# Decoder layer: VectorE turns the cross-attention keys in squares of 32, the scores contract over 32 partitions, and the attention loops are written out

## What is computed

```python
x = _layernorm(x + _L0_attn_ref(x, ...), axis=-1)      # a state-space mixer, 128 heads
x = _layernorm(x + _L0_xattn_ref(x, ctx_4096), axis=-1)
x = _layernorm(x + _L0_ffn_ref(x, ...), axis=-1)       # 512x512 base + top-2 of 8 low-rank experts
...
def _L0_xattn_ref(query, key):
    a = jnp.einsum('bqd,bkd->bqk', query, key)
    e = jax.nn.softmax(a, axis=-1)
    c = jnp.einsum('bqk,bkd->bqd', e, key)
    return c
```

## Time and profile before

| | us |
|---|---|
| median of 3 runs | 1640.62 (1637.20 to 1644.48) |
| the profiled execution | 1644.59 |
| its span, first to last instruction | 1642.8 |
| mean granted TensorE clock | 0.981 |

### The profile page before, as it was taken

How to read it: one execution, slowest core, us unless ns; L and a number is a source line. 1 busy time by engine, 2 the same in 40 slices (tenths; PEclk the granted TensorE clock), 3 DMA queues, 4 the chain that set the end, 5 groups by cost and what they waited for, 6 DMA issues and landing times. The chain is left out here.

```text
span 1642.8 us, 26149 instructions
## 1 busy us (share of the span) xinstructions
PE 1569.8 (96%) x9596; PEld 1249.5 (76%) x9596; DVE 1027.0 (63%) x1279; ACT 720.9 (44%) x947; POOL 648.1 (39%) x395
## 2 busy tenths in 40 slices
PE   5999999999999999999999999999975899999996
PEld 5888888989898888889898988888864455444442
DVE  5785775678477847757774777587465245444544
ACT  5664635545563646355364636554531122222120
POOL 5364545545454745446364636454451000000000
PEclk9999999999999999999999999999987899999998
DMA  4421212213121222122121213121159177776600
GB/s 141 122 88 59 78 52 82 66 48 88 55 75 59 88 65 65 59 75 78 37 88 59 88 47 99 49 65 61 47 120 226 68 156 162 162 162 159 153 15 12
DMA packets 50380, 142.77 MB, mean 87 GB/s; under 512 B 9248, under 2 KB 9376, under 8 KB 48160
## 3 DMA queue, kind: packets, MB, share of 16 engines
q1 hardware_dynamic: 50288, 141.41, 31.8%
HBM read 137.03 MB, written 4.13 MB: 86 GB/s over the span
## 5 line engine op out<-in xcount | busy, mean ns | idle before, releaser
L1106 PE MATMUL bank<-h_hi,w_hi 128*128 128x448 f32 x1152 | 338.4, 375 | 2.7 <-DVE conv L755 2.7
L755 DVE SCALAR_TENSOR_TENSOR conv<-bank,conv_w,conv 128x880 f32<-128x880 f32 (+2 forms) x240 | 268.0, 1117 | 102.0 <-ACT conv L554 83.4
L1106 PE MATMUL bank<-h_lo,w_hi 128*128 128x448 f32 x1152 | 327.8, 366 | 0.0
L1106 PE MATMUL bank<-h_hi,w_lo 128*128 128x448 f32 x1152 | 327.0, 365 | 0.0
L425 POOL TENSOR_TENSOR y_lo<-yg,y_hi 128x896 fp32r<-128x896 f32 x64 | 135.8, 2121 | 331.2 <-ACT y_hi L581 331.2
L1106 PEld LDWEIGHTS bank<-h_lo,w_hi 128*128 128x128 f32 x1152 | 217.0, 188 | 17.2
L1106 PEld LDWEIGHTS bank<-h_hi,w_lo 128*128 128x128 f32 x1152 | 216.7, 188 | 17.4
L441 POOL TENSOR_TENSOR mixw<-decay,cbm 64x896 f32<-64x896 f32 x64 | 163.6, 2556 | 166.2 <-ACT decay L614 95.3
L1106 PEld LDWEIGHTS bank<-h_hi,w_hi 128*128 128x128 f32 x1152 | 208.3, 189 | 24.8 <-DVE conv L755 3.7
L409 POOL TENSOR_TENSOR w_lo<-w_raw,w_hi 128x512 fp32r<-128x512 f32 x144 | 193.7, 1346 | 77.3 <-ACT w_hi L520 76.5
L796 DVE TENSOR_TENSOR hd_dt<-bank,dt_j 128x512 f32<-128x512 f32 x128 | 82.4, 685 | 182.9 <-PE bank L1136 182.7
(11 more groups left out here) (159 smaller groups left out, 2265.9 us busy)
## 6 DMA issues: line engine op xcount, KB each, us to landing
keys<-in_context SPq DMA_DIRECT2D x16, 2688.0 KB
w_raw<-in_w_in SPq DMA_DIRECT2D x144, 256.0 KB, 2.9
decay<-cs_scratch SPq DMA_DIRECT2D x128, 196.0 KB
wo_raw<-in_w_out SPq DMA_DIRECT2D x64, 256.0 KB, 2.7
keys<-in_context SPq DMA_DIRECT2D x16, 312.0 KB
acc<-in_x SPq DMA_DIRECT2D x1, 1792.0 KB, 8.5
x_scratch<-acc SPq DMA_DIRECT2D x7, 256.0 KB, 25.4
out<-z SPq DMA_DIRECT2D x16, 112.0 KB
```

The source lines that it names most:

```text
L755: v.scalar_tensor_tensor(out=dst[:, :, sh:LEN], in0=src[:, :, 0:LEN - sh], scalar=conv_w[:, bass.ds(col, 1), TAPS - 1 - sh], in1=dst[:, :, ...
L1106: last = mm(place, w[:, k * P:(k + 1) * P], x[:, k, half * HALF:(half + 1) * HALF], start=(k == 0 and i == 0), stop=(k == KT - 1 and i == 2))
```

## The change

The mixer stays as it is. From its end on:

- Keys come in units: a third of a pair, 4 of the 12 blocks of both sequences, as one transfer of 125 rows, each of 2 x 8 KB (`load_unit`); for the first six units 3 more rows, so that all 128 partitions hold numbers. A ring of six slots holds two pairs.
- DVE turns the keys from SBUF to SBUF in squares of 32 x 32 (`keys_part`, 12 instructions a pair, 128 partitions x 1024 numbers each). A square stays in its own quarter of the partitions, so a quarter (`row`) of `keysT` holds 32 channels of the keys of that quarter.
- The scores are 128 products a pair over 32 partitions, 384 columns (348 in the last quarter). Quarter `row` works with row group `row` of the array and writes bank `row`; the softmax runs over the four banks, of which three numbers a block in the last are preset to -3e38.
- Every quarter needs the queries of each 32 channels, so ACT writes 16 copies of 32 partitions x 512 numbers a pair (`queries`).
- PE's transposes of the keys and their copies on ACT and DVE are gone. ACT now also copies x2T and two of the three `probsT` banks. x1 goes straight from `acc` to `x1p`; the scratch in DRAM is gone. All pairs are written out, no loop.

The core of the diff:

```diff
-                    for lo, hi in ((0, 112), (112, KP)):
-                        sp.dma_start(keys[lo:hi, u, q].rearrange("p j d -> p (j d)"),
-                                     A["context"][n * 4 + 2 * u + q, lo:hi, :]).then_inc(keys_loaded[u], 16)
+            def load_unit(unit):
+                u, r = unit // KR, unit % KR
+                src = A["context"][2 * u:2 * u + 2, :, r * UNIT:(r + 1) * UNIT]
+                sp.dma_start(piece(unit)[0:KP], src.rearrange("q p n -> p q n")
+                             ).then_inc(unit_loaded[slot_of(unit)], 16)
+                if unit < RING:
...
             sp.wait_ge(s["w_used"], GROUPS * WT)
+            load_unit(0)
+            load_unit(1)
             sp.wait_ge(s["cb_done"], GROUPS)
...
+            load_unit(2)
             sp.wait_ge(s["x1p_zero"], 1)
...
+            load_x1(0)
...
+            for unit in range(KR, RING):
+                load_unit(unit)
+
+            for u in range(PAIRS):
+                if 1 <= u < PAIRS - 1:
+                    for r in range(KR):
+                        sp.wait_ge(s["v_mm"], KR * (u - 1) + r + 1)
+                        load_unit(KR * (u + 1) + r)
+                if u + 1 < PAIRS:
+                    load_x1(u + 1)
+                if u >= 2:
+                    store(u - 2)
...
+                for c in range(4):
+                    for row in range(4):
+                        last = a(qT[SQ * row:SQ * (row + 1), :, c, :], src[SQ * c:SQ * (c + 1)], ACT.Copy)
+                last.then_inc(s["q_set"], 1)
...
+            def keys_part(u, r, half):
+
+                wait_unit(dve, KR * u + r)
+                at_least(dve, s["s_mm"], 2 * (u - 1) + half + 1)
+                for q in range(2):
+                    v.transpose(
+                        keysT[:, q, 8 * half:8 * half + 8, KB * r:KB * (r + 1), :].rearrange("p b j i -> p j b i"),
+                        piece(KR * u + r)[:, q, :].rearrange("p (j h b i) -> p h j b i", j=KB, h=2, i=SQ)[:, half]
+                    ).then_inc(s["kT_set"], 1)
...
+                    if not live and st == 1:
...
+                        keys_part(0, 0, 0)
+                        keys_part(0, 0, 1)
                     if st == 1 and not first:
                         group_squares(g)
...
+                for b in range(NB):
+                    if b == 0:
+                        pe.wait_ge(s["kT_set"], 12 * u + 10)
...
+                    for row in range(4):
+                        lo, n = SQ * row, min(SQ, KP - SQ * row)
+                        for q in range(2):
+                            last = mm(scores[PAD * q:PAD * (q + 1), row, :].rearrange("p (j i) -> p j i", i=SQ)[:, :, 0:n],
+                                      qT[lo:lo + SQ, b // 4, b % 4, PAD * q:PAD * (q + 1)],
+                                      keysT[lo:lo + SQ, q, b, :, 0:n], start=(b == 0), stop=(b == NB - 1))
...
+            for u in range(PAIRS):
+                score(u)
+                if u >= 1:
+                    turn_x2(u - 1)
+                    feed_forward(u - 1)
+                for r in range(KR):
+                    turn_probs(u, r)
+                values(u, 0)
+                values(u, 1)
+                if u >= 1:
+                    turn_hw(u - 1)
+                values(u, 2)
+                if u >= 1:
+                    lora(u - 1)
+                if u + 1 < PAIRS:
+                    turn_queries(u + 1)
```

More of the change, by code:

```diff
@@ L36 @@
 KJ, KP = 12, 125
+KR, KB = 3, 4
+RING = 6
+UNIT = KB * DM
+SQ, NB = 32, 16
+LOWEST = -3.0e38
 EXP, RANK = 8, 16
@@ L218, in real, with slot_of, piece, wait_unit @@
             return ap.rearrange("p (b i) -> p b i", b=SEQS)[:, :, 0:LEN]
+        def slot_of(unit):
+            return unit % RING
+        def piece(unit):
+            slot = slot_of(unit)
+            return ring_a[:, slot] if slot < KR else ring_b[:, slot - KR]
+        def wait_unit(eng, unit):
+            eng.wait_ge(unit_loaded[slot_of(unit)], 16 * (unit // RING + 2))
+        def x1_pieces(u):
+            return sum(1 + ((2 * u + q) * LEN // P != ((2 * u + q + 1) * LEN - 1) // P) for q in range(2))
+        def x1_landed(u):
+            return 16 * sum(x1_pieces(k) for k in range(u % 2, u + 1, 2))
+        def at_least(eng, semaphore, value):
+            if value > 0:
+                eng.wait_ge(semaphore, value)
         block = ctx.enter_context(nc.Block())
@@ L324, in store @@
[L324 to L327, removed]
+            def load_unit(unit):
[4 more added lines that the diff above has]
+                if unit < RING:
+                    sp.dma_start(piece(unit)[KP:P], src[:, 0:P - KP, :].rearrange("q p n -> p q n")
+                                 ).then_inc(unit_loaded[slot_of(unit)], 16)
@@ L353, in _ @@
                 sp.dma_start(dst, src).then_inc(s["ffn_loaded"], 16)
[L354 to L371, removed]
+            for unit in range(KR, RING):
[9 more added lines that the diff above has]
+                    store(u - 2)
+            for u in range(PAIRS - 2, PAIRS):
+                store(u)
             for i in range(2):
@@ L673, in first_norm @@
                   scale=rstd1[:, t:t + 1]).then_inc(s["x1_set"], 1)
[L675 to L684, removed]
@@ L950, in norm2_sum, with link @@
-            def norm2_sum(n, u, cell):
-                wait(dve, s["exps_done"], 2, n, u + 1)
-                link(v.reciprocal(S["rsum"], S["esum"]), n, cell)
-                wait(dve, s["pv_done"], 2, n, u + 1)
-                v.scalar_tensor_tensor(out=x2[:, u, :], in0=pv, scalar=S["rsum"], in1=x1p[:, u, :],
+            for r in range(1, KR):
+                for half in range(2):
+                    keys_part(0, r, half)
+            steps = [1]
+            def link(ins):
+                ins.then_inc(s["dstep"], 1)
+                steps[0] += 1
+                dve.wait_ge(s["dstep"], steps[0])
@@ L1082, in _ @@
+            norm3_sum(PAIRS - 1)
+            norm3_stats(PAIRS - 1)
+            norm3_apply(PAIRS - 1)
         @block.tensor
@@ L1187, in sum_squares, with turn_queries @@
                 last.then_inc(s["ss_done"], 1)
+            def turn_queries(u):
+                pe.wait_ge(x1_loaded[u % 2], x1_landed(u))
+                at_least(pe, s["q_set"], u)
+                if u == 0:
+                    pe.wait_ge(s["yres_done"], GROUPS * CT)
+                for k in range(KT):
+                    last = tr(turn[:, k * P:(k + 1) * P], x1p[:, u % 2, k * P:(k + 1) * P], ident[:])
+                last.then_inc(s["q_tr"], 1)
             def second_half(g):
@@ L1202, in second_half @@
                         sum_squares(g)
+                    if t == TT - 1 and not has_group(g):
+                        turn_queries(0)
             def first_half(g):
@@ new lines, in turn_probs, with values @@
+            def turn_probs(u, r):
+                if r == 0:
+                    pe.wait_ge(s["exps_done"], u + 1)
+                for j in range(KB):
+                    last = tr(bank[:, r, j * P:(j + 1) * P], probs[:, KB * r + j, :], ident[:])
+                last.then_inc(s["pT_tr"], 1)
+            def values(u, r):
+                wait_unit(pe, KR * u + r)
+                if r == 0:
+                    at_least(pe, s["z2_done"], u)
+                    pe.wait_ge(s["pT_evac0"], u + 1)
+                else:
+                    pe.wait_ge(s["pT_evac12"], 2 * u + r)
+                for j in range(KB):
+                    for q in range(2):
+                        last = mm(pv[PAD * q:PAD * (q + 1), :], probsT[0:KP, KB * r + j, PAD * q:PAD * (q + 1)],
+                                  piece(KR * u + r)[0:KP, q, j * DM:(j + 1) * DM],
+                                  start=(r + j == 0), stop=(r == KR - 1 and j == KB - 1))
+                last.then_inc(s["v_mm"], 1)
```

516 lines of the change are left out of this document (222 added, 294 removed).

## The result

The changed kernel takes **1715.95 us** (median of 4, 1694.8 to 1728.95) against 1640.46 (median of 4, 1637.2 to 1644.48): slower, as forecast in sign, and within the range. The ratio on record, **1.0367, interval 1.0331 to 1.0403**, is that of the two faster executions of the change (1694.8 and 1708.8), since the other two lie more than 1.5% above the fastest. The profiled execution took 1723.11 us with a span of 1721.4 (before: 1644.59 and 1642.8), so its span is compared with the 1677.5 of the prediction's axis.

A forecast was written before the change was run, and what follows sets the result against it. Key transfers on five engines were to bound the kernel: at 49.0 us a pair, pair 7's query rows land at 1612.5; query chain, scores, values and tail lead to 1677.5, plus 1.8 minus 4 gives 1675 us; range 1612 to 1760.

The forecast's parts named there:

- 125 rows divide only into 5 engines: Key transfers: rows are dealt out in equal whole numbers, so each transfer reaches five of 16 engines, share near 0.31.
- 49.0 us a pair: Key transfers: three units at 126 GB/s take 48.8 us, with query rows and stores 49.0, above PE's 44.
- first queries turned: Start of attention: the first query rows land at 1264 us, behind units 0 to 2 of the keys.
- last scores, from there: Last pair: turned queries at the slow clock and ACT's query copies take 11.2 us before scores start.
- to the last value: PE's work in a pair from last score to last value, feed-forward and values included: 18.7 us.
- tail: After the last value: 22.9 us before, 1.5 less because ACT now copies x2T, so 21.4 us.
- so the queue never runs dry: Key ring: slots come free in time, values ending some 40 us after a pair's query rows land.
- rival B: Key transfers: five engines at a lower rate each; 1776 us at 20 GB/s, 1976 at 14.2; chance 0.12.
- the order of the steps of a pair: PE in every pair: waits some 6 us for `x1p`, then 9.7 us for `qT` on ACT.
- the row groups: Score products: four row groups run side by side, bounds 10.7, 14.1 and 43 us; 11.0 taken, plus 2.7 for the clock.
- DVE is no bound: Key turning on DVE: 12 pieces at 1.1 us; DVE's work 24 to 37 us of a pair.
- Rival A: Key transfers use nearly all engines and are never late; 44.0 us a pair, result 1626 us; chance 0.14.

The follow-up runs named there:

- run 2: The changed kernel with each unit of keys issued as 124 rows and 1 row instead of 125; 1788.78 us.
- run 1: The changed kernel with each unit of keys issued as 112 rows and 13 rows, nothing else altered; 1628.21 us, ratio to before 0.9895.
- run 3: The kernel before the change, with a sequence's keys issued as one transfer of 125 rows instead of 112 and 13; 1701.11 us.
- run 4: The changed kernel, 125-row units kept, next pair's queries turned before this pair's values and their rows issued ahead of the last units; 1688.12 us.
- run 5: The changed kernel with units of 112 and 13 rows and the next pair's queries turned before this pair's values; 1549.82 us, ratio to before 0.9444.
- run 6: The kernel of run 1 with all 16 score steps of one quarter before the next quarter, instead of quarters side by side; 2115.66 us.

## Why the prediction was right, and where its sum was off

**Right: what decides.** "125 rows divide only into 5 engines" is what shares of 0.32, 0.26 and 0.68 showed in the change and in runs 2 and 1.

**The step that was mis-sized: 49.0 us a pair, from five engines that move 25.2 GB/s each and never wait.** The rate came from a transfer on 13 or more engines, with the argument that five would get in each other's way less. In the windows of the change an engine moved 115/(0.32 x 16) = 22.5 to 123/(0.32 x 16) = 24.0, in the last one shown 24.2. Where the missing 44 us of the span are (the traced execution is 28 us above the fastest, of which there is no trace):

| step | forecast | measured | more |
|---|---|---|---|
| first queries turned | 1264 | 1270.56 | 6.6 |
| second | 1318.5 | 1331.56 | 6.5 |
| eighth, six pairs on | 6 x 49.0 | 1658.24 - 1331.56 = 6 x 54.4 | 32.7 |
| last scores, from there | 11.2 | 10.8 | -0.4 |
| their length | 13.7 | 12.5 | -1.2 |
| to the last value | 18.7 | 18.1 | -0.6 |
| tail | 21.4 | 21.8 | 0.4 |

All but a trifle lies in three rows of one term. The six pairs took 57.6, 61.0, 54.2, 51.7, 52.5 and 49.7 us, so the last all but reached the 49.0.

The trace has the duration of every row that a DMA engine moves, and these durations split the term. Between 1331.56 and 1658.24 a row of keys, 8 KB, took 313 ns at the median, which is 26.2 GB/s and more than the 25.2, but 339 ns on average, 24.1 GB/s, since some rows take twice as long. 150 rows an engine and pair make 50.9 us instead of 48.8: 2.1 of the 5.4 us that a pair took more. In the rest, 54.4 - 50.9 = 3.5 us a pair, the five engines were not all moving keys. The forecast had 0.2 us there, for query rows and stores, and with "so the queue never runs dry" nothing for waiting. But the five don't end together. At the end of the last keys one engine alone is at work, 1 of 16:

```profile
1610.00:1634.00 24.00, 14.04 (x260) 8.21 (x260) 10.62 (x17) 9.65 (x17) 1.10 (x2) 0.68 0.32 130
1644.00:1656.00 12.00, 7.93 (x34) 2.35 (x29) 4.06 (x5) 0.00 (x0) 0.00 (x0) 1.00 0.07 28
```

PE's last wait for `x1p` ends at 1658.24, behind this engine's rows. Earlier pairs show the same: from 1534 to 1540 the share is 0.17, and the next keys are issued at 1538.63, once the first values of the pair are done. So four engines stood idle while the fifth finished. In the last pair the slowest engine set the time; that it did so in the earlier ones too is inferred, since the trace doesn't name the engine of a row.

Why some rows take longer, and why one engine falls behind, no run settles. The kernel's own compute engines alone are not the reason: from 1376 to 1388 and from 1496 to 1502 PE, DVE, ACT and POOL all stand still and the share is 0.32, yet 111 GB/s move in the first stretch and 132 in the second. Nor is it the number of engines alone: 24 KB rows on five gave 25.6 (run 3), 8 KB rows on four 24.3 to 25.5 in windows of 50 us (run 2), and the very transfers of the change 25.0 to 25.2 in five such windows of run 4 and 124/(0.34 x 16) = 22.8 in the sixth. It also moves from one execution to the next, 34 us between the fastest and the slowest of the change, where the kernel before has 7. The range given for the forecast alone, 1655 to 1700, had allowed 46 to 52 a pair, and the profiled execution had 54.4. The whole range held because it had been drawn up to the milder rival B, 20 GB/s an engine; the measured rate lies between the two, nearer the forecast's.

**Right: the order of the steps of a pair.** PE waits for `x1p` first, 12.5 us on average where some 6 were expected, then 9.7 us for `qT`, as the forecast said; the copies are 588 ns each (0.61 from start to start was taken).

**Right: the row groups.** 11.0 us and 2.7 for the clock against 12.0 to 13.5, 12.6 on average; the block at full clock is 10.56, so the first bound (10.7) is the true one and the clock costs 2.1 on average. The Trainium skill, "TensorE: Matmul & The Clock Gate", section "Packing small matmuls — row/col tiling", has 3.07 times for four row tiles, which would have made 13.9: the 10.56 us of run 5 speak against it here. Run 6 shows that the gain hangs on the order.

**Right: DVE is no bound.** 12 pieces at 1.22 us (1.1 taken), 4.62 for four in a row, so 1.16 each when nothing interrupts. Its new wait ahead of `group_squares`, 4.88 us, was longer than the 2.5 taken, and hidden as said, since SP's weights followed at 1257.95, before at 1257.76:

```profile
1232.05 4.62 DVE L897 STREAM_TRANSPOSE keysT<-ring_a 128x1024 f32<-128x1024 f32 x4 [4.88 <-DMA ring_a<-in_context]
```

**Rival A's sum, tried by run 1,** came to 1626 for 1628.21, in part by luck, since errors cancel. The values of pair 0 end at 1293.4 instead of 1299, the last values of the seven further pairs lie 45.3 us apart, not 44.0, and the tail is 20.5, not 21.4. A pair without a hole is 42.3 (turned queries at 1433.08 and 1475.37), 1.7 below the sum: scores 13.0 for 13.7, to the last value 18.1 for 18.7, the chain 9.7 for 10.0. What the sum lacked is a hole inside the score block:

```profile
1518.88 0.60 PE L1213 MATMUL bank<-ident,x1p 128*128 128x128 f32 x4
1529.16 12.09 PE L1295 MATMUL bank<-keysT,qT 32*64 32x384 f32 x235 [9.68 <-ACT qT L704]
1543.97 2.58 PE L1295 MATMUL bank<-keysT,qT 32*64 32x384 f32 x21 [2.72 <-issue]
...
1550.26 5.51 PE L1319 MATMUL bank<-wbT,x2T 128*128 128x512 f32 x8
1555.61 1.47 PE L1334 MATMUL bank<-ident,probs 128*128 128x128 f32 x12
```

PE stands 2.72 us for nothing that the profile shows, and the feed-forward behind it takes 5.51 us instead of 3.60, at the lower clock again: this pair takes 50.0.

## What to carry to other kernels

- Before a transfer is made larger or fewer, look at the number of its outer rows: 112 and 13 rows in two transfers used all DMA engines, 125 rows in one used five of them, and neither the bytes nor the instruction count tell the difference. A flat DMA share at k/16 is its mark. The time of such a transfer is that of its slowest engine, not of the mean rate.
- Work taken off the engine that sets the time was also the cover of a serial chain (here turned queries, sixteen copies, scores): move that chain beside other work in the same edit. Products for different row groups must be neighbours in the order to run side by side.

## What the runs showed of the hardware

- **The clock stayed at its lower level under a busy PE.** With products of one row group after the other PE was busy 20.00 of 20.00 us at a granted clock of 0.50 (run 6), and it did not rise in the whole block of 72.8 us, which followed a pause of 9.7 us. The same products with the row groups side by side, after the same pause, had 0.50 in the first 4 us, 0.89 in the next 4 and 1.00 after that (run 1, from 1443.4). That PE's time is full doesn't mean that the clock is.
- **Holes in a row of products, only beside wide transfers.** Gaps marked "issue" stand inside the score blocks of run 1 (six of eight, 1.03 to 2.84 us) and of run 5 (seven of eight, 0.56 to 2.97 us), six of them after the same number of records in both, and none in the last pair, when no keys are loading. The change, run 2 and run 4 have the same products written out in the same way, and none of their 24 blocks has such a gap; there 11 or 12 engines are left free. So the gap goes with the transfers over all engines. The trace lists transfers of a second kind beside the program's, "instruction", and they tell what PE waits for: in all 13 gaps one of them, 16 KB on queue 8, ends 1.3 to 1.7 us before PE goes on. In run 1 it starts 5.9 to 12.8 us after the block's first product, in the same blocks of the change 1.7 to 7.7 us after it, and in the last pair 1.1 us in both. So PE's own instructions come 4 to 6 us later beside wide transfers, and in six of seven blocks that is too late. No run took the written-out loops away, so that a loop would be free of the gaps is not shown.
- **The rate of one DMA engine** was 22.5 to 25.9 GB/s in windows of 50 us with four or five at work, and the sixteen together moved 205 to 207 GB/s at shares of 0.92 to 0.96, some 14 each (run 5), as the 14.2 of the earlier trace rows: three times the engines gave 1.7 times the rate. A row of 8 KB took 339 ns on average in the change and 572 in run 1. The number of engines alone does not set it: the weights of the earlier trace rows moved 25.2 each at a share of 0.83.
- A copy of 32 partitions x 512 numbers on ACT costs 588 ns, one of 128 partitions (`probsT`) 595, both in the change: the sixteen copies cost as much as sixteen of full height.
